# One low part of a block by GpSimd, from exponentials written in place over the quad's scores

## The reference

```
q, k, v = Wq x + bq, Wk x + bk, Wv x + bv          # q and k have 32 channels, v has 256
att     = softmax(q^T k / sqrt(32), over the keys)  # 4096 x 4096 per image
out     = gamma * (v att^T)
result  = Wf [out ; x] + bf                         # Wf is 256 x 512
```

## Time and profile before

| | |
|---|---|
| Median of 3 runs | 1999.03 us (1997.72 to 2000.24) |
| Profiled execution, its own time | 1999.28 us |
| its span, first to last instruction | 1997.5 us |
| Granted TensorE clock, mean | 0.998 |
| Busy share of PE, DVE, ACT, POOL | 99%, 85%, 86%, 65% |

### The profile page before, as it was taken

The page is one execution under the profiler, slowest core; times in us unless marked ns, Lnnn a source line. Parts: engine busy times, 40 slices in busy tenths (PEclk is TensorE's granted clock), DMA queues, the critical chain, the costliest instruction groups (busy, mean ns, idle before and its releaser), DMA issues.

```text
span 1997.5 us, 46306 instructions
## 1 busy us (share of the span) xinstructions
PE 1971.6 (99%) x15720; PEld 1931.8 (97%) x15720; DVE 1689.5 (85%) x2669; ACT 1715.5 (86%) x2309; POOL 1290.0 (65%) x578
## 2 busy tenths in 40 slices
PE   9999999999999999999999999999999999999998
PEld 8899999999889999999989999999998999999998
DVE  6888989887788889898678888898967898888985
ACT  7888888887888898888788888988868888889885
POOL 0477777777057777777605777777760687777775
PEclk9999999999999999999999999999999999999999
DMA  4311111110321111111032111111104111111111
GB/s 139 85 20 19 16 21 22 21 21 12 122 71 23 20 17 16 21 21 22 12 127 66 23 22 19 18 16 21 22 12 132 38 23 22 21 20 17 17 22 17
DMA packets 297815, 69.69 MB, mean 35 GB/s; under 512 B 280528, under 2 KB 281296, under 8 KB 297680
## 3 DMA queue, kind: packets, MB, share of 16 engines
q1 hardware_dynamic: 297408, 67.97, 15.8%
q10 hardware_dynamic: 272, 0.07, 0.0%
HBM read 34.41 MB, written 33.55 MB: 34 GB/s over the span
## 4 chain that ended last, share of the span: by engine, by line
PE 86%; DVE 6%; issue 4%; ACT 3%; POOL 1%; DMA 0%; DVEq 0%; POOLq 0%; ACTq 0%; SPq 0%
PE ps_o L389 70%; PE ps_s L381 11%; PE ps_p L269 3%; DVE top L596 2%; ACT queries L465 1%; POOL raw L764 1%; PE ps_o L269 1%; ACT hi L444 1%; DVE val_lo L684 1%; PE ps_s L286 1%; DVE lo L583 1%; PE ps_s L269 0%; DVE lo L640 0%; ACT raw L450 0%; DVE top_j L601 0%
## 5 line engine op out<-in xcount | busy, mean ns | idle before, releaser
L764 POOL TENSOR_TENSOR raw<-raw,top_m 128x1024 f32<-128x1024 f32 x508 | 1209.1, 2415 | 444.2 <-DVE raw L635 261.8
L640 DVE TENSOR_TENSOR lo<-ps_p,hi 128x1024 fp32r<-128x1024 f32 x512 | 623.6, 1218 | 159.7 <-ACT ps_p L531 147.0
L596 DVE TENSOR_TENSOR top<-ps_s,top 128x512 f32<-128x512 f32 x960 | 658.9, 686 | 56.7 <-ACT raw L450 7.1
L389 PE MATMUL ps_o<-val_hi,hi 128*128 128x258 f32 x4096 | 659.9, 283 | 7.1 <-DVE val_lo L684 5.4
L389 PE MATMUL ps_o<-val_lo,hi 128*128 128x256 f32 x4096 | 653.3, 281 | 0.0
L524 ACT ACTIVATE hi<-raw 128x1024 fp32r<-128x1024 f32 x512 | 544.6, 1064 | 123.8 <-PE ps_o L389 115.7
L389 PE MATMUL ps_o<-val_hi,lo 128*128 128x258 f32 x4096 | 604.3, 285 | 3.9 <-DVE lo L640 3.8
L531 ACT ACTIVATE ps_p<-raw 128x1024 f32<-128x1024 f32 x512 | 520.9, 1017 | 67.4 <-DVE lo L640 67.4
L450 ACT ACTIVATE raw<-ps_s 128x512 f32<-128x512 f32 x1024 | 554.4, 596 | 24.3 <-PE ps_s L381 1.6
L389 PEld LDWEIGHTS ps_o<-val_hi,hi 128*128 128x128 f32 x4096 | 563.4, 190 | 8.8 <-DVE val_lo L684 6.7
L389 PEld LDWEIGHTS ps_o<-val_lo,hi 128*128 128x128 f32 x4096 | 561.0, 189 | 0.0
(11 more groups left out here) (67 smaller groups left out, 1022.6 us busy)
## 6 DMA issues: line engine op xcount, KB each, us to landing
xf<-x SPq DMA_DIRECT2D x32, 512.0 KB, 3.9
conv_d<-conv_st SPq DMA_DIRECT2D x64, 256.0 KB, 2.1
result<-conv_d SPq DMA_DIRECT2D x512, 32.0 KB, 1.9
out<-result SPq DMA_DIRECT2D x512, 32.0 KB, 1.6
raw<-wf2T SPq DMA_DIRECT2D x1, 256.0 KB, 3.9
raw<-wv SPq DMA_DIRECT2D x1, 256.0 KB, 4.1
raw<-wf1T SPq DMA_DIRECT2D x1, 256.0 KB, 4.6
raw<-wkqT ACTq DMA_DIRECT2D x1, 64.0 KB, 2.7
```

The lines of the kernel that those rows point to most:

```text
L389: last = nc.tensor.matmul(ps_o[:, i, 0:width], p[:, t % 2, jl * I + i * P:jl * I + (i + 1) * P], v[:, j, 0:width], start=opens and jl == 0 ...
L596: nc.vector.tensor_tensor(top[:, new], scores, top[:, new if half else old], ALU.max).then_inc(max_done, 1)
L640: nc.vector.tensor_tensor(lo[:, t % 2], ps_p[:].rearrange("p h n -> p (h n)"), hi[:, t % 2].bitcast(F32), ALU.subtract).then_inc(lo_done, 1)
L764: nc.gpsimd.tensor_tensor(raw[:, slot], raw[:, slot], top_m[:, r].unsqueeze(1).broadcast_to((P, JQ, I)), ALU.subtract).then_inc(sub_done, 1)
```

## The change

In every block that has a next one, the low part of quad 5 goes from VectorE to GpSimd. GpSimd can't read PSUM. So ScalarE writes the full-precision exponential of quad 5 over the quad's scores in its `raw` slot instead of into ps_p, and GpSimd subtracts hi from it. GpSimd does so after its subtractions for quads 6 and 7 and before it waits for the next block's maximum. VectorE skips this quad's `split_p` and goes from the chain of maxima straight to the fold of the scores of quad 16.

```
-            def exponential(Q, t, slot):
+            def exponential(Q, t, slot, in_place=False):
 
                 if not (isinstance(Q, int) and Q + t == 0):
                     act.wait_ge(lo_done, Q + t)
-                nc.scalar.activation(ps_p[:].rearrange("p h n -> p (h n)"), raw[:, slot].rearrange("p j i -> p (j i)"),
+                scores = raw[:, slot].rearrange("p j i -> p (j i)")
+                nc.scalar.activation(scores if in_place else ps_p[:].rearrange("p h n -> p (h n)"), scores,
                                      ACT.Exp, scale=SCALE).then_inc(p_done, 1)
...
-                        exponential(Q, t + 1, (QUADS * r + t + 1) % SLOTS)
+                        exponential(Q, t + 1, (QUADS * r + t + 1) % SLOTS, t == 4 and not last_block)
...
                     if t < QUADS - 1 or not last_block:
-                        split_p(Q, t + 1)
+
+                        if t != 4 or last_block:
+                            split_p(Q, t + 1)
...
+            def split_p(Q, t, slot):
+
+                pool.wait_ge(p_done, Q + (t + 1))
+                nc.gpsimd.tensor_tensor(lo[:, t % 2], raw[:, slot].rearrange("p j i -> p (j i)"), hi[:, t % 2].bitcast(F32),
+                                        ALU.subtract).then_inc(lo_done, 1)
...
                         if t == QUADS - 2:
+                            split_p(snap(pool, B * QUADS), 5, (QUADS * r + 5) % SLOTS)
                             pool.wait_ge(m_done, B + 2)
                         subtract_top((r + 1) % OUTS, slot)
```

## The result

The changed kernel takes 2012.1 us (median of 4 runs, 2011.27 to 2012.96) against 1999.6 for the kernel before. The ratio is 1.0064, with a 95% interval of 1.0047 to 1.0082: slower by 12.5 us, where 13.3 were forecast. The profiled execution took 2012.96 us; its span is 2011.1, 13.6 us longer than the span before.

The account below looks back on a forecast made before the run. TensorE was taken to bound the kernel, with only 12.3 us of waiting to gain. The terms 52 x 0.31 + 4 x 0 - 4 x 0.7 = +13.3 us on 1999.0 gave 2012.3 us, range 1997 to 2027.

Parts of the forecast that it names:

- The old wait: TensorE before lo of quad 5: wait plus slow restart, 0.12 us in a common block, 12.3 us in all, the most gainable.
- The exponential in place: ScalarE's exponential of quad 5 into SBUF takes 1.06 us instead of 1.01, within idle time, so free.
- GpSimd's subtraction: GpSimd's low part of quad 5 takes about 2.4 us, 309.07 to 311.47; output rounding may add to it.
- The chain stops at the copy: VectorE's chain of maxima is held at its copy until 0.13 us before GpSimd's end; top_m at 312.96 instead of 311.30.
- third case: VectorE's chain is held already at the reduction, top_m at 313.42; part of a longer-hold rival, about 2040 us, chance 0.12.
- The middle case: The copy is the first VectorE chain instruction held, top_m at 312.96; the forecast case, 2012.3 us, chance 0.50.
- Lo of quad 7 is what is late next: TensorE waits 0.34 us for VectorE's lo of quad 7, restart 0.09; net +0.31 us in each of 52 blocks.
- First blocks: nothing: In each image's first block TensorE loses about 0.45 us before and about the same after: change 0.
- Block 14: -0.7: In block 14 lo of quad 5 leaves 0.1 of 1.07 us, lo of quad 7 costs 0.25: -0.7 us each.
- The sum: Common blocks 16.1, first blocks 0, block 14 -2.8: +13.3 us in all.

Follow-up runs that it names:

- three kernels: Changed kernel with copies and maxima as reductions, 0.9934; changed kernel with quad 16's fold before the copy, 0.9935; kernel before with VectorE's lo of quad 5 inside the chain, 0.9933.
- the run with the reduction: Changed kernel with only the chain's first copy written as a reduction of length 1: 1997.89 us, ratio to the kernel before 0.9992.

## Why the prediction was right

The mechanism was right at each step; that the sum came within 1 us of the measurement was partly luck.

- *The old wait is all that can be gained.* Right: three kernels end at 0.9933 to 0.9935. Its size was 13.7 us and not 12.3, as above.
- *The exponential in place is free.* Right: 1.04 us, and a ratio of 1.0000 alone.
- *GpSimd's subtraction takes 2.4 us, the output's type adds nothing.* Right: 2.41.
- *The chain stops at the copy, and goes on 0.13 us before GpSimd's end.* Right: 1.82 us in place of 0.17, and 0.14. The reduction isn't held (third case out), the two-input maximum would have been the next (the run with the reduction). The middle case was chosen with no row on a copy or a reduction beside GpSimd; its cost over the next one, 0.20 us a block, was decisive: it is nearly the whole difference between slower and no change. (The prediction lets GpSimd run across seven of the chain's instructions; by its own times it is eight, from the reduction at 309.22 on. Nothing in it depends on this.)
- *Lo of quad 7 is what is late next.* Right: TensorE waits there, 0.30 + 0.11 us for 0.34 + 0.09, and nowhere else in such a block. But the net of 0.31 us was too large: in the mean over 52 blocks it was 27.257 - 27.012 = 0.245 us, because the new wait costs 0.40 us against a block of 26.86 and the old one had cost 0.15.
- *First blocks: nothing.* Right. TensorE's group in image 0's first block comes at 102.84 where 102.54 was due; with the restart that is 0.41 us, about the 0.45 that it lost at quad 5, and over the four first blocks the difference is 0.03 us.
- *Block 14: -0.7.* Roughly right. In the rows of the changed kernel, the group with lo of 5 follows the lead at once (477.45 + 0.48 = 477.93 against 477.97), and the group of quad 7 lasts 0.58 us (to 483.46) without a wait:

```profile
477.45 0.63 PE L389 MATMUL ps_o<-val_lo,hi 128*128 128x256 f32 x4
477.97 1.23 PE L389 MATMUL ps_o<-val_hi,lo 128*128 128x258 f32 x8
...
482.88 0.75 PE L389 MATMUL ps_o<-val_hi,lo 128*128 128x258 f32 x4
483.46 0.64 PE L389 MATMUL ps_o<-val_hi,hi 128*128 128x258 f32 x4
```

  That is 0.04 + 0.10 + 0.10 = 0.24 us left of 1.07, so -0.8.
- *The sum.* In part luck. The forecast terms, 16.1 + 0 - 2.8 = 13.3 us, measure 12.7 + 0 - 3.3 = about 9.5 us. The median moved by 12.5 because the changed kernel's executions also had a lower granted clock, for which the prediction has no term: three more low-clock stretches make 4.5 us in the profiled pair. Waits of 9.5 us alone would still have been slower by 0.5%, and inside the range.

## What to carry to other kernels

An engine's idle gap isn't free to be filled only because no semaphore stands in the way: here GpSimd's gap lay exactly beside VectorE's small SBUF-to-SBUF instructions, and work put into it stopped a 0.17 us copy for 1.8 us. Before moving work to GpSimd, list VectorE's instructions beside the new place by where their operands lie, and look for a stretched duration (the largest beside the median) where the two already touch. If the work must go there, put PSUM-fed instructions into the stretch or write the small ones as reductions; and first see whether a reordering on one engine doesn't give the same. And before a sum of waits is set beside a difference of under 1%, compare the granted clock of the two kernels' runs: here it stood for about 3 of 12.5 us.

## What the runs showed of the hardware

- A copy of 8 columns from SBUF to SBUF is held by GpSimd like a large two-input instruction: 1.82 us against 0.17. So 8 columns are not too few to be held, and the copy didn't get in between two GpSimd instructions in a row (1.36 us beside two memsets of 0.95).
- A reduction over an axis of length 1 makes the same move in 0.16 us and isn't held.
- VectorE holds GpSimd as well: behind a two-input lo of 1.18 us GpSimd's first subtraction took about 0.9 us longer.
- A subtraction on GpSimd with one tile as both inputs and output took 1.89 us, with two different inputs 2.41.
- Even a wait of 0.03 to 0.04 us on TensorE adds about 0.1 us to the group behind it (1.06 instead of 0.97 us for 8 matmuls).
- Behind the same wait of 1.8 us at an image's start, the granted clock fell to about half (1.2 GHz) for some 3.4 us in some images and not in others (17 or 18 matmuls in 3.5 us instead of 29). Each time cost about 1.5 us.
